# Attention on one core: a third probabilities buffer, the denominators products moved behind the values products, the division one slot later, the gate's choice at slot 44

## The reference, cut to what matters

```
x = x + 0.5 * ffn0(layernorm(x))          # sqrt((n cos)^2 + (n sin)^2)
x = x + attention(layernorm(x))           # 16 heads of 64, 512 keys
x = x + 0.5 * ffn0(layernorm(x))
...
scores = softmax(xq @ xk * scale)         # per head, over 512 keys
out = (scores @ xv) @ Wo
```

## Time and profile before

| | us |
|---|---|
| median of 3 runs (lowest, highest) | 2524.42 (2524.15, 2532.09) |
| span of the profiled execution | 2524.8 |
| TensorE busy | 2163.5 (86%) |
| VectorE busy | 1827.8 (72%) |
| GpSimd busy | 1455.5 (58%) |
| ScalarE busy | 1410.7 (56%) |

### The profile page before, as it was taken

How to read it: one execution, slowest core, us unless ns; L and a number is a source line. 1 busy time by engine, 2 the same in 40 slices (tenths; PEclk the granted TensorE clock), 3 DMA queues, 4 the chain that set the end, 5 groups by cost and what they waited for, 6 DMA issues and landing times. The chain is left out here.

```text
span 2524.8 us, 39953 instructions
## 1 busy us (share of the span) xinstructions
PE 2163.5 (86%) x14226; PEld 994.3 (39%) x14226; DVE 1827.8 (72%) x4240; ACT 1410.7 (56%) x2651; POOL 1455.5 (58%) x1264
## 2 busy tenths in 40 slices
PE   3689989989889889989989998569898899898878
PEld 1223333333323333323323322236566566665534
DVE  5777777777777777777777773358888888887668
ACT  2166566566566566566566566254555655556234
POOL 3366666665665665665665645146555656565358
PEclk9799999999999999999999999689999999999789
DMA  3221211112112112112112120100000000000033
GB/s 116 55 49 38 50 36 46 47 35 51 42 34 51 43 34 56 38 34 58 35 34 59 31 69 9 30 13 22 26 22 26 26 22 26 22 18 14 14 100 109
DMA packets 86598, 103.70 MB, mean 41 GB/s; under 512 B 10240, under 2 KB 68736, under 8 KB 86272
## 3 DMA queue, kind: packets, MB, share of 16 engines
q1 hardware_dynamic: 86400, 101.16, 15.3%
HBM read 29.55 MB, written 20.97 MB: 20 GB/s over the span
## 5 line engine op out<-in xcount | busy, mean ns | idle before, releaser
L347 DVE TENSOR_REDUCE mS<-ps 128x1 f32<-128x512 f32 x1024 | 676.9, 681 | 301.8 <-PE ps L724 297.3
L506 ACT ACTIVATE pr<-ps 128x512 f32<-128x512 f32 x1024 | 585.9, 597 | 383.7 <-PE ps L708 365.6
L579 POOL TENSOR_TENSOR prs<-pr 128x512 f32<-128x512 f32 x384 | 487.3, 1288 | 243.3 <-ACT pr L506 243.3
L708 PE MATMUL ps<-qst,kst 97*128 97x512 f16 x1024 | 397.2, 391 | 53.3 <-ACT pr L506 52.2
L724 PE MATMUL ps<-kst,qst 96*128 96x512 f16 x1024 | 400.4, 392 | 36.6 <-DVE mS L347 25.7
L746 PE MATMUL ps<-pr,vt 128*32 128x512 f32 x2048 | 279.6, 619 | 0.0
L708 PEld LDWEIGHTS ps<-qst,kst 97*128 97x128 f16 x1024 | 99.1, 98 | 419.3 <-ACT pr L506 307.3
L583 POOL TENSOR_TENSOR terms<-terms 128x512 f32<-128x512 f32 x128 | 162.4, 1268 | 69.3 <-DVE terms L340 69.3
L340 DVE TENSOR_TENSOR terms<-ps,shared 128x512 f32<-128x512 f32 x256 | 173.1, 678 | 34.9 <-POOL lo L588 29.7
L588 POOL TENSOR_TENSOR lo<-terms,hi 128x512 f16<-128x512 f32 x128 | 148.0, 1156 | 76.9 <-ACT hi L486 76.9
L724 PEld LDWEIGHTS ps<-kst,qst 96*128 96x128 f16 x1024 | 101.1, 99 | 150.4 <-DVE mS L347 80.1
(11 more groups left out here) (267 smaller groups left out, 4399.2 us busy)
## 6 DMA issues: line engine op xcount, KB each, us to landing
qst<-hi SPq DMA_DIRECT2D x128, 128.0 KB, 2.4
kst<-hi SPq DMA_DIRECT2D x128, 128.0 KB, 2.4
qst<-lo SPq DMA_DIRECT2D x64, 128.0 KB, 2.4
kst<-lo SPq DMA_DIRECT2D x64, 128.0 KB, 2.4
x<-in_q SPq DMA_DIRECT2D x16, 256.0 KB, 2.8
shared<-in_rope SPq DMA_DIRECT2D x1, 4096.0 KB, 14.4
x<-yold SPq DMA_DIRECT2D x16, 256.0 KB, 2.5
n<-kept SPq DMA_DIRECT2D x16, 256.0 KB, 2.1
```

Of the source, the lines that this page charges most:

```text
L347: v.tensor_reduce(mS[:, b % 2, t, s:s + 1], ps[:, 2 + n % 2, :], AX, ALU.max).then_inc(S["s_read"], 1)
L506: a.activation(pr[:, s % 2, g, :], ps[:, g % 2, :], ACT.Exp, scale=ATT_SCALE).then_inc(S["exp"], 1)
L579: g.tensor_tensor(prs[:, c, :], pr[:, 0, c, :], pr[:, 1, c, :], ALU.add).then_inc(S["prs"], 1)
L708: mm(ps[:, g % 2, :], kst[:, h, P * kt:P * kt + P], qst[:, h, :], start=True, stop=True).then_inc(S["st"], 1)
```

## The change

Four things are done together. `pr` holds three steps' probabilities in place of two, and the waits of the exponentials are rewritten for it: step s now needs step s-3 to be read, not s-2. `denominators_lag` goes from 3 to 5, so that each denominators product stands in the same slot as a values product, right behind it (slots 13, 21, 29, 37, 45, 53); the direct ones stand at 57 (two of them), 61 and the end. The parts of `divide` stand one slot later (22 to 24, 38 to 40, 54 to 56). The gate's choice goes from slot 41 to 44 and the counting from 45 to 49.

```diff
-    "xn2": 31, "turn2": 36, "evac2": 35, "gate": 37, "gate_in": 37, "next_hi": 50, "next_lo": 55, "gate_top": 41, "gate_count": 45,
+    "xn2": 31, "turn2": 36, "evac2": 35, "gate": 37, "gate_in": 37, "next_hi": 50, "next_lo": 55, "gate_top": 44, "gate_count": 49,
-    "denominators_lag": 3, "maxima": 5,
+    "denominators_lag": 5, "maxima": 5, "divide": 6, "direct": {57: (12, 13), 61: (14,)},
...
+RING = 3
+PAIRED = 12
...
-        pr = sb("pr", [P, 2, NT, SEQ])
+        pr = sb("pr", [P, RING, NT, SEQ])
...
+        def probabilities(b, s):
+            return pr[:, (HEADS * b + s) % RING]
...
-                        if is_att(i) and s % NG == 1 and s > NG and t:
-                            divide(i - 2, s // NG - 1, t - 1)
+                        j, part = divmod(q - AT["divide"], NG * NT)
+                        if is_att(i) and 1 <= j and part < 3:
+                            divide(i - 2, j - 1, part)
...
-                    if g == 0 and head >= 2:
-                        act.wait_ge(S["pv"], head - 1)
-                    if 2 <= s < HEADS - 2 and s % 2 == 0:
-                        act.wait_ge(S["prs"], NG * ((HEADS // 2 - 2) * b + s // 2 - 1) + g + 1)
...
+                    if head >= RING:
+                        pb, old = (head - RING) // HEADS, (head - RING) % HEADS
+                        if g == 0:
+                            act.wait_ge(S["pv"], head - RING + 1)
+                        if old < PAIRED and old % 2 == 0:
+                            act.wait_ge(S["prs"], NG * (PAIRED // 2 * pb + old // 2) + g + 1)
+                        if old >= PAIRED and g == 0:
+                            act.wait_ge(S["dd"], (HEADS - PAIRED) * pb + old - PAIRED + 1)
...
-                        if is_att(i) and s > HEADS - NT and t == 3:
-                            denominators_directly(i - 2, s - 1)
+                        if is_att(i) and q in AT["direct"]:
+                            for k in AT["direct"][q]:
+                                denominators_directly(i - 2, k)
```

More of the change, by code:

```diff
@@ L495, in exponentials @@
                     head = HEADS * b + s
-                    if g == 0 and head >= 2:
-                        act.wait_ge(S["pv"], head - 1)
-                    if 2 <= s < HEADS - 2 and s % 2 == 0:
-                        act.wait_ge(S["prs"], NG * ((HEADS // 2 - 2) * b + s // 2 - 1) + g + 1)
[L500 to L503, removed]
+                    if head >= RING:
[6 more added lines that the diff above has]
+                            act.wait_ge(S["dd"], (HEADS - PAIRED) * pb + old - PAIRED + 1)
                     n = SLOTS * b + NG * s + g
                     act.wait_ge(S["st"], n + 1)
-                    a.activation(pr[:, s % 2, g, :], ps[:, g % 2, :], ACT.Exp,
+                    a.activation(probabilities(b, s)[:, g, :], ps[:, g % 2, :], ACT.Exp,
                                  scale=ATT_SCALE).then_inc(S["exp"], 1)
@@ L578, in add_pair @@
                         pool.wait_ge(S["dn"], pairs)
-                    g.tensor_tensor(prs[:, c, :], pr[:, 0, c, :], pr[:, 1, c, :], ALU.add).then_inc(S["prs"], 1)
+                    g.tensor_tensor(prs[:, c, :], probabilities(b, 2 * n)[:, c, :], probabilities(b, 2 * n + 1)[:, c, :],
+                                    ALU.add).then_inc(S["prs"], 1)
                 def rotated(b, p):
@@ L745, in values @@
                         h = NG * g + j
-                        ins = mm(ps[DH * g:DH * g + DH, 6, :], vt[:, kt, DH * h:DH * h + DH], pr[:, s % 2, g, :],
+                        ins = mm(ps[DH * g:DH * g + DH, 6, :], vt[:, kt, DH * h:DH * h + DH], probabilities(b, s)[:, g, :],
                                  start=kt == 0, stop=kt == NT - 1, skip_group_check=True)
@@ L763, in denominators_directly @@
                     for g in range(NG):
-                        ins = mm(ps[DH * g:DH * g + DH, 7, :], w["ones"][:, 0:DH], pr[:, s % 2, g, :],
+                        ins = mm(ps[DH * g:DH * g + DH, 7, :], w["ones"][:, 0:DH], probabilities(b, s)[:, g, :],
                                  start=kt == 0, stop=kt == NT - 1, skip_group_check=True)
```

## The result

| | before | after |
|---|---|---|
| median, us (lowest, highest; 4 runs each) | 2524.28 (2522.86, 2532.09) | 2650.59 (2633.67, 2655.1) |
| ratio after/before | | 1.0461, 95% interval 1.0429 to 1.0494 |
| profiled execution: span, us | 2524.8 | 2651.8 |

Slower, and outside the range: the medians are 126 us apart where 24 were forecast, and the ratio in the table is 4.6%. The four executions of the change lie between 2633.67 and 2655.1 us, and the profiled one, at 2654.76, is among the slowest, so what is read from its trace is a little more than the median holds. In the attention phase 122.6 us were lost (1454.6 from its first score product to its last, 1577.2 after): 8.47 in each of the ten iterations that I averaged (93.93, now 102.40), 7.3 in the last (66.6, now 73.9).

The account below looks back on a forecast made before the run. No engine bounds all 64 slots; TensorE has most to do. Terms of -0.25, +1.8 and +0.7 make +2.25 us an iteration, +29 over 13, less 5: 2524.8 + 24 = 2548 us, range 2506 to 2571.

Parts of the forecast that it names:

- list of what would show it: Signs: L762 0.86 us behind L753 without GpSimd wait, half clock at slot 29 or 37, L563 1 to 2 us later.
- Slots 47 to 53: Block leaves slot 51, removing 2.1 us; ScalarE's numerators copy holds the values product of slot 53, so 0.4 us gain remains.
- The term of the clock: Half-clock falls on slot 29 and slots 36 and 37 cost 1.8 us an iteration, bounds 0 and 3.1.
- the -0.25: Slots 28 to 37: first projection comes earlier, mean change -0.25 us an iteration, before the added clock falls.
- the 0.33: Slots 38 to 46: GpSimd's later start costs 0.33 us an iteration, replacing TensorE's 0.37 us delay at slot 46.
- The division: Its first part enters VectorE's full stretch; slot 40's multiplication meets GpSimd's rotary add, about 0.1 us, left out of the sum.
- Slots 54 to 63: Four-slot stretch with the division inside: stalls of 1.24 us, less 0.47 saved by two seams, net 0.77 us loss.
- Slots 0 to 27, nothing: Moving blocks from 11 and 19 to 13 and 21 only shifts TensorE inside waits for ScalarE: no cost.
- The ring, nothing: Three probabilities buffers cost nothing, as exponentials at slots 49 to 51 wait behind a rotary cast anyway; they allow later blocks.
- the 0.73 us ahead of the block of slot 27: A wait attributed to ScalarE's table loads; with another of 1.04 behind it, removing the block was to free nothing.
- The rival "slower still": Both clock falls each iteration (3.1 us) and the multiplication blocked for a whole add: +46, 2570 us; chance 0.17.
- -5 in the first and last iterations: First and last two iterations project little, so waits of blocks at 43 and 51 go for good: -5 us.

Follow-up runs that it names:

- e5: Changed kernel with only the gate's counting back at slot 45 (choice stays at 44): 2649.25 us.
- e8: Changed kernel with the denominators blocks of slots 29 and 37 back at 27 and 35 and the counting back at 45: 2595.0 us.
- e13: Changed kernel with reciprocal deviations ahead of GpSimd's add of slot 28, directs back at 55, 59, 63, gate at 41 and 45; six pairings kept: 2581.64 us.
- e3: Changed kernel with four additional float32 products that nobody reads at each of slots 27 and 35: 2601.77 us.
- e7: Changed kernel with the second layer norm's reciprocal deviations ahead of GpSimd's first add of slot 28: 2595.73 us.
- e6: Kernel before with only the gate's choice at slot 44 and the counting at 49: 2530.17 us.
- e17: Changed kernel with the denominators blocks of slots 45 and 53 back at 43 and 51: 2597.8 us.
- e16: Changed kernel with both the filling products at slots 27 and 35 and the reciprocal deviations ahead of GpSimd's add of slot 28: 2598.24 us.
- e10: Kernel before with the ring of three and the division one slot later; blocks and gate where they were: 2549.3 us.
- e1: Changed kernel with denominators blocks back at slots 11 to 51 and directs at 55, 59, 63; ring, division and gate stay changed: 2550.55 us.
- e18: Changed kernel with filling products at slots 27 and 35 and the denominators blocks of 45 and 53 back at 43 and 51: 2586.94 us.

## Why the prediction was wrong

The direction and most of the mechanisms it named were right, and so was most of its list of what would show it: no wait for GpSimd ahead of L762, 0.86 us between the blocks, half clock on slot 29 in all ten iterations, the add of slot 28 released by TensorE, the reciprocal 2.7 us later. The sizes were not. Two terms of the sum carry the miss.

- *"Slots 47 to 53: ... Of 2.1 us removed, 0.4 is left."* This step failed, by a term that it left out. Slots 51 to 53 went from 5.90 to 8.63 us, a loss of 2.73 where I had a gain of 0.4: 3.1 of the 6.2 us an iteration that I was off by. The block's own move was read rightly: in e5, e8 and e13, whose counting isn't at 49, these slots take 5.03 us, 0.87 less than before. But the counting, moved from 45 to 49, got no cost and no reason for having none. There GpSimd's adds block it, and the projection of slot 51 waits for VectorE behind it: 2.0 us (5.03 to the 7.0 of iterations of e3 and e7 without the third fall). The third fall, over a TensorE emptied by that wait and by the block's leaving, is the other 1.6 (7.0 to 8.63). With the block at its old slot the same counting costs 0.29 (e6). So neither move costs much alone, and the two together cost 2.73; e17 shows that returning this block and that of 45 is worth 3.44 us an iteration, 2.4 of it from slot 48 on.
- *"I take 0.7 x 1.5 + 0.45 x 1.6 = 1.8 us ... 3.1 (both each time)."* The term of the clock was mis-sized. With the -0.25 and the 0.33 I had +1.9 for slots 28 to 46; the same slots measured +4.35 (30.57 to 34.92). The fall of slot 29 came every time, lasted 6.8 us and not 3.4, and a second one came each time too. e3, e7 and e16 put what this chain costs at 3.4 us, some 3.1 of it in slots 28 to 47 (e3, e7). My upper bound priced each fall by iterations that had one.
- *The division:* 0.3 us at slots 38 to 46 and a share of the 0.77 behind it; 1.68 alone (e10). I named 0.1 us for the multiplication in slot 40, from the mean of all four in an iteration. That mean got 0.2 us longer (983 ns), and in slot 40 the multiplication takes 1.37 us in every one of the ten iterations, 0.70 more than in slot 39 before: it starts in the middle of GpSimd's first rotary add, where before it fell into a gap of GpSimd's. The Trainium skill (SBUF — State Buffer, Who interferes with whom) has a VectorE instruction with two SBUF inputs contend with a GpSimd one that reads SBUF, so that one is blocked for the other's whole length. The trace agrees best at the counting, 0.23 us grown to 1.22; at the multiplication it shows about half of an add of 1.27. The step also missed the second user of the denominators' bank, the direct product.
- *Slots 54 to 63:* 0.77 predicted, 13.52 to 14.89 measured, +1.37. The pairing of the directs is 0.3 of it (e17 against e1 from slot 48 on, 24.81 and 24.49).
- *Slots 0 to 27, nothing:* 38.67 and 38.69. Right, but beside the ring alone (38.56) 0.13 is lost.
- *The ring, nothing:* -0.3%, just at the bound of what can be told, with iterations 0.07 us shorter.
- *Readings:* the 0.73 us ahead of the block of slot 27 is ended by GpSimd's add, not by a table load; nothing in the sum hangs on it. The rival "slower still" took 5 us for a multiplication blocked for a whole add, where 1.27 us in 13 iterations make 16.5.
- *-5 in the first and last iterations:* the last alone is 7.3 us longer. No run took it apart.

Taken from one kernel to the next, the steps lead from before to after: 93.93, ring -0.07, later division +1.68, gate +0.02, e1 to e18 +2.42 (the pairings that e18 keeps, with the filling), and +4.42 for what the filling and the two blocks back return together: 102.40. The chance of "slower" was the largest, and yet its cases ended at 2571: the rival "slower still" put both falls of the list in each iteration, but no third fall at a place that I had booked as a gain.

Open stays why the falls lock as they do: the changed kernel repeats 102.40 us with all three at the same places in every iteration of the profiled execution, while e17 wanders between 96.4 and 100.4. The Trainium skill (TensorE: Matmul & The Clock Gate, part 1) has activity release the throttle; that agrees with 1.27 and 1.13 us busy of 3.40 ahead of two of the falls. Which of several thin places brings the fall, the runs don't show. Two sum buffers for GpSimd, which would unhook the add from the block without reordering, were not tried.

## What to carry to other kernels

Two moves that cost little or even gain alone can be dear together: here a block that left a slot, and a counting that put a wait for another engine into that same slot. A matrix product that stands inside such a wait is free, whatever wait its own row shows; before moving it, find what the next instruction behind it waits for with all the other edits in place, and give every moved instruction a term in the sum, if only of nothing with a reason. A producer that now waits for its consumer takes everything behind it on its queue along: count that queue, not the add. Where an engine's clock depends on its load, price a thinned stretch with all falls that a later chain can bring, and expect one mend to help and two not to add.

## What the runs showed of the hardware

- One fall of 3.4 us costs between nothing and 1.6 us by where it lies: before's iterations take 93.13 us with a fall 39 us into them and 94.75 with one at 48.6. In e18 10.2 us at half clock cost 4.3 (100.7 against 96.4). The third fall of the changed kernel costs 1.6 (8.63 against 7.0 in slots 51 to 53).
- Adding products that nobody reads to TensorE made the changed kernel faster (e3): the ratio went from 1.0461 to 1.0299, the iteration from 102.40 to 98.98 us.
- A VectorE instruction of 64 elements a partition took five times as long (225 to 1221 ns) beside a GpSimd add, at slot 49 (e6 too) as at slot 45 (e5, e8).
- A VectorE multiplication of 128x512 took 1.37 us in slot 40, where a GpSimd add was running, and 0.67 in slot 39 of the kernel before.
